# A transformer block with experts on one core: the causal mask moved to GpSimd, second expert product turned, token step and first expert rearranged

## The reference, cut to what matters

```python
h = concatenate([tok(x), txt], axis=1)                 # (32, 165, 256)
n = layernorm(h)
q, k, v = heads(n @ Wq + bq), heads(n @ Wk + bk), heads(n @ Wv + bv)
att = einsum('bhtd,bhsd->bhts', q, k) / sqrt(16)
att = where(key <= row and key % 4 != 3, att, -inf)
h = h + merge(softmax(att) @ v) @ Wp + bp
xn = rmsnorm(layernorm(h)) * norm_weight               # (5280, 256)
probs = softmax(xn @ router_w.T + router_b)
gates, idx = top_k(probs.T, 660)                       # per expert
hmid = gelu(xn[idx] @ fc1_w.T + fc1_b)                 # (8, 660, 1024)
ye = hmid @ fc2_w.T + fc2_b                            # (8, 660, 256)
out = scatter_add(ye * gates) / sum of a token's gates
h = h + out
```

## Time and profile before

| | us |
|---|---|
| median of 3 runs | 911.26 (909.67 to 915.45) |
| the profiled execution | 917.64 |
| its span | 915.8 |
| PE busy | 781.5 (85%) |
| DVE busy | 626.4 (68%) |
| ACT busy | 336.8 (37%) |
| POOL busy | 290.2 (32%) |

### The profile page before, as it was taken

One profiled execution on the slowest core, in us unless ns is written; L12 is line 12 of the kernel. 1 busy time (PEld: TensorE's weight loads), 2 busy tenths in 40 slices (PEclk: granted clock), 3 DMA queues, 4 the chain that ended last, 5 costly groups with the idle time before them and its releaser, 6 DMA issues. The chain is left out here.

```text
span 915.8 us, 19773 instructions
## 1 busy us (share of the span) xinstructions
PE 781.5 (85%) x7384; PEld 712.9 (78%) x7384; DVE 626.4 (68%) x1487; ACT 336.8 (37%) x729; POOL 290.2 (32%) x312
## 2 busy tenths in 40 slices
PE   4789999999999999989998621259999999999997
PEld 2668888888888888878887421259989998999997
DVE  1326768777677686776866567767877877878662
ACT  0203433343343333333332136116346264472560
POOL 3011122121221212222111120431653835637434
PEclk8879999999999999999999855559999999999999
DMA  9954574654765546644464170210442633415122
GB/s 296 260 80 62 65 114 89 94 77 83 114 99 87 83 84 103 108 78 80 84 98 72 45 242 0 92 31 13 95 127 26 147 96 60 131 23 101 31 30 31
DMA packets 81645, 83.22 MB, mean 91 GB/s; under 512 B 36249, under 2 KB 75911, under 8 KB 81212
## 3 DMA queue, kind: packets, MB, share of 16 engines
q1 hardware_dynamic: 68948, 67.82, 37.5%
q0 software_dynamic: 11584, 10.96, 7.7%
q10 hardware_dynamic: 1032, 3.37, 1.1%
HBM read 35.56 MB, written 16.22 MB: 57 GB/s over the span
## 5 line engine op out<-in xcount | busy, mean ns | idle before, releaser
L622 ACT ACTIVATE r_arena<-ps_all 126x660 f32<-126x660 f32 x128 | 92.3, 721 | 109.3 <-PE ps_all L815 109.3
L1166 DVE TENSOR_REDUCE mx<-ps_all 128x4 f32<-128x504 f32 (+1 forms) x160 | 104.7, 667 | 23.2 <-PE ps_all L791 22.8
L1177 DVE RECIPROCAL r_arena<-ps_all 128x165 f32<-128x165 f32 x64 | 76.1, 1189 | 57.1 <-PE ps_all L830 57.0
L541 POOL DMA_INDIRECT xe<-xn_rows,r_arena x48 | 69.4, 1446 | 133.2 <-DVE r_arena L1452 105.9
L1058 PE MATMUL ps_all<-W_hi,hT_hi 128*110 128x256 f32 x384 | 108.9, 284 | 0.0
L1058 PE MATMUL ps_all<-W_hi,hT_lo 128*110 128x256 f32 x384 | 107.7, 280 | 0.0
L1058 PE MATMUL ps_all<-W_lo,hT_hi 128*110 128x256 f32 x384 | 107.6, 280 | 0.0
L815 PE MATMUL ps_all<-Qp,Kp 98*126 98x166 f32 x512 | 102.5, 315 | 0.0
L554 POOL DMA_INDIRECT out<-r_arena x48 | 88.6, 1846 | 38.2 <-issue 35.8
L791 PE MATMUL ps_all<-Kp,Qp 96*65 96x56 f32 (+1 forms) x512 | 92.2, 297 | 0.0
L1490 DVE TENSOR_TENSOR hT_lo<-r_arena,hT_hi 128x330 fp32r<-128x330 f32 x128 | 63.3, 502 | 41.0 <-ACT r_arena L699 40.8
(11 more groups left out here) (172 smaller groups left out, 1821.6 us busy)
## 6 DMA issues: line engine op xcount, KB each, us to landing
H<-w SPq DMA_DIRECT2D x16, 1024.0 KB, 6.5
Qp<-q_hi SPq DMA_DIRECT2D x64, 166.0 KB, 3.9
Kp<-k_hi SPq DMA_DIRECT2D x128, 63.0 KB, 4.1
Qp<-q_lo SPq DMA_DIRECT2D x32, 166.0 KB, 4.5
out<-H SPq DMA_DIRECT2D x16, 330.0 KB
xn_rows<-r_arena SPq DMA_DIRECT2D x16, 330.0 KB
Kp<-k_lo SPq DMA_DIRECT2D x64, 63.0 KB, 4.0
H<-h SPq DMA_DIRECT2D x1, 3360.0 KB, 25.5
```

Source lines behind the costliest of these rows:

```text
L541: pool.indirect_dma_start(xe[0:A, a, :], None, xn_rows, bass.IndirectOffsetOnAxis(tok[0:A, u, a:a + 1], 0), bounds_check=NTOK - 1).then_in ...
L622: act.activation(PT[0:S, g, :, :].rearrange("p (k h) t -> p k h t", k=2), pair[:, :, :, 0:T], ACT.Exp, scale=float(HD) ** -0.5).then_inc(e ...
L1166: dve.tensor_reduce(dst, src, AX.X, ALU.max).then_inc(max_ready, 1)
L1177: dve.reciprocal(rS[:, c, :], bank(2 + c)[:, T:2 * T]).then_inc(rs_sum, 1)
```

## The change

- Masks: `mask_keys` and its products are gone from `key_scores`. On GpSimd `zero_future(b, g)`, an `affine_select` over `PT`, zeroes the entries of future keys after the exponential; `mix_values` waits for it (`causal_done`) and no longer for the exponential itself.
- Second products turned: `fc2` holds 128x128 pieces of W2 and streams 330 columns of the hidden rows, four quarters of 24 products (half j, features c). ACT adds the bias while it copies a quarter to `yS` (`evacuate`), PE transposes back (`output_rows`, three tiles after the third quarter, three after the first two blocks of the next expert's fc1), and DVE only multiplies by the slot weight.
- Token numbers: `slot_values(e+1)` comes after two of 16 blocks and `tokens(e+1)` after two features (`SV_AT = 1`).
- First expert: high and low parts of its weights are made in search steps 3 to 8; `first_tokens` starts with each third of the one-hots; gathers signal in two halves (for every expert), and `fc1(0)` takes the first half of the rows for four features first (`hidden_order`).
- The biases `b2` come with `vecs`, the eight broadcast loads on SP are gone; `pack_max` stands ahead of `store_h` on SP; PE's and ACT's expert loops are written out.

```diff
-SV_AT, TOK_AT = 4, 6
+SV_AT, SV_AT_FIRST = 1, 4
+def hidden_order(e):
+    if e == 0:
+        return [(f, j) for j in range(2) for f in range(KFF // 2)] + \
+               [(f, j) for f in range(KFF // 2, KFF) for j in range(2)]
+    return [(f, j) for f in range(KFF) for j in range(2)]
...
+            def zero_future(b, g):
+                pool.wait_ge(exp_done, 4 * b + g + 1)
+                apart(pool)
+                pool.affine_select(PT[0:S, g, :, :], PT[0:S, g, :, :], [[0, 4], [STEP - 1, T]], ALU.is_ge, 0.0,
+                                   base=STEP - 2, channel_multiplier=-STEP).then_inc(causal_done, 1)
...
+                if 3 <= step < 3 + KD:
+                    k = step - 3
+                    act.wait_ge(w1_in[0], 16)
+                    act.activation(W1_hi[:, k, :], W1[:, 0, k, :], ACT.Copy).then_inc(w1_hi_ready, 1)
+                if 3 + KD <= step < 3 + KD + KFF // 2:
...
             def mix_values(b, c):
-                pe.wait_ge(exp_done, 4 * b + 2 * c + 2)
+                pe.wait_ge(causal_done, 4 * b + 2 * c + 2)
...
+            def fc2(e, quarters):
+                for q in quarters:
+                    j, c = q // 2, q % 2
...
+                    for i, (w, h, f) in enumerate(terms):
...
+                        mm = pe.matmul(bank(4 + c)[:, 0:HALF], w[:, f, c * 128:(c + 1) * 128], h[:, f, cols],
                                        start=(i == 0), stop=(i == len(terms) - 1))
...
+            for e in range(NE):
+                split = 2 * (SV_AT if e else SV_AT_FIRST)
+                fc1(e, range(0, 2))
+                if e >= 1:
+                    output_rows(e - 1, range(3, NA))
+                fc1(e, range(2, split))
+                if e + 1 < NE:
+                    slot_values(e + 1, True)
+                fc1(e, range(split, 2 * KFF))
+                fc2(e, range(0, 2))
+                if e + 1 < NE:
+                    expert_transposes(e + 1, range(0, 2))
+                fc2(e, range(2, 3))
+                output_rows(e, range(0, 3))
+                if e + 1 < NE:
+                    expert_transposes(e + 1, range(2, 4))
+                fc2(e, range(3, 4))
+            output_rows(NE - 1, range(3, NA))
...
-                    hidden(e, u, seen, range(0, TOK_AT))
+                    hidden(e, u, seen, range(0, 1))
+                    weigh(e - 1, v, range(3, NA), e > 1)
+                    hidden(e, u, seen, range(1, SV_AT + 1))
                     tokens(e + 1, v, again)
-                    hidden(e, u, seen, range(TOK_AT, KFF))
+                    hidden(e, u, seen, range(SV_AT + 1, KFF))
```

More of the change, by code:

```diff
@@ L499, in _ @@
                 n, u = divmod(b, 2)
+                has_s = 0 <= b < B
                 if u == 0:
@@ L718, in _ @@
-            act.wait_ge(h_ready, 16 * (NE - 1))
-            gelus(NE - 1)
+                for n, (f, j) in enumerate(hidden_order(e)):
+                    act.wait_ge(fc1_done, 16 * e + n + 1)
+                    apart(act)
+                    if 16 * e + n >= 4:
+                        act.wait_ge(h_ready, 16 * e + n - 3)
+                        apart(act)
+                    act.activation(hT_hi[:, f, j * HALF:(j + 1) * HALF], bank(n % 4)[:, 0:HALF], ACT.Gelu,
+                                   bias=b1_s[:, e, f:f + 1]).then_inc(gelu_done, 1)
+                    act.activation(h_raw[:, n % 4, :], bank(n % 4)[:, 0:HALF], ACT.Gelu,
+                                   bias=b1_s[:, e, f:f + 1]).then_inc(gelu_done, 1)
@@ new lines, in evacuate @@
+            def evacuate(e, quarters):
+                for q in quarters:
+                    j, c = q // 2, q % 2
+                    act.wait_ge(fc2_done, 4 * e + q + 1)
+                    if e >= 1 and c == 0:
+                        act.wait_ge(yt_done, NA * (e - 1) + 3 * j + 3)
+                    act.activation(yS[:, c, j * HALF:(j + 1) * HALF], bank(4 + c)[:, 0:HALF], ACT.Identity,
+                                   bias=b2_s[:, e, c:c + 1]).then_inc(y_evac, 1)
+            act.activation(warm[:, :], kf("row"), ACT.Gelu)
@@ L1031, in fc1 @@
                 if 0 in parts:
[L1032 removed]
+                    pe.wait_ge(xeT_ready, 4 * e + 2)
                     pe.wait_ge(w1_split, KD * e + KD)
[L1034 to L1045 removed]
@@ L1062, in _, with output_rows @@
+            def output_rows(e, tiles):
+                for a in tiles:
+                    at_bank, at_col = y_place[a]
+                    if a % 3 == 0:
+                        pe.wait_ge(y_evac, 4 * e + 2 * (a // 3) + 2)
+                    for c in range(KD):
+                        mm = pe.transpose(bank(at_bank)[0:A, at_col + c * 128:at_col + (c + 1) * 128],
+                                          yS[:, c, a * A:(a + 1) * A], ident)
+                    mm.then_inc(yt_done, 1)
             first_tokens()
```

258 lines of the change are left out of this document (122 added, 136 removed).

## The result

The changed kernel takes 917.91 us (median of 20 runs, 914.74 to 921.89); the kernel before, 913.51 in 20 runs beside it (909.67 to 919.82). The ratio is 1.0049, with a 95% interval of 1.0030 to 1.0068: half a per cent slower, inside the 1% that the prediction takes for no change. The forecast was 897, 14 us faster. The profiled execution took 917.84 us, its span is 916.1.

What follows compares the result with a forecast made beforehand. PE was taken to bound attention's even rounds and the experts, DVE the odd rounds. -12.8 +1.0 +1.2 -7.2 +0.5 +3.5 = -13.8 us took 917.64 to 904, and the median 911.26 to 897; range 868 to 930.

Steps and rivals of the forecast that it cites:

- Masks and the end of attention: Attention: mask products replaced by GpSimd selects, -12.8 us over 16 pairs of rounds; last round's norm-weight products behind selects, +1.0.
- The 0.3 us by which selects hold DVE: Odd attention rounds: GpSimd selects block DVE's two-port ops, adding 0.3 us to the DVE chain.
- the 0.35 us of the odd round: Odd attention rounds: PE waits 0.35 us for the last select before the second half of the mixing products.
- Search: Threshold search: GpSimd's low parts of the first expert's weights hold DVE there, net +1.2 us, bounds 0 to +6.
- the token products: First expert: 16 of 48 token products start behind each third of the one-hots, 32 beside DVE: -3.1 us.
- The rest of the first expert: First expert: fc1 on half the rows -1.3 us, slot values and early gather -0.3, fc2 by quarters -2.5.
- fc1 starts on half the rows: First expert: fc1 starts on half the rows, without the second half's low parts: -1.3 us.
- Experiments 1 to 6: No such term in the prediction.
- PE waits 3.3 us. Everything won is gone: Experts 1 to 6: the token step waits for an earlier scatter; PE's 3.3 us wait leaves +0.1 an expert.
- The last expert and the end: PE ends 1.1 us earlier, but six late scatters queue on GpSimd and lengthen the end by 4.7: +3.5 us.
- the missing token wait: Rival, experts 1 to 6: no wait for the scatter, six experts each 3.3 us shorter, 877 us; chance 0.20.
- The slow select: Rival, attention: selects of 1.4 us become the bound, attention +29 us, 939 us; chance 0.25.

Runs made afterwards that it cites:

- experiment 8: The changed kernel with three buffers of token numbers, but masks as before (a mask product on PE per bank, no select on GpSimd): 895.07 us.
- late conversions: Three-buffer kernels with the high parts of the first expert's weights made after the search, as in the kernel before; without further change 876.87 and 880.85 us.
- experiment 10: Three-buffer kernel with the first expert's hidden products in the other experts' order, each block for both halves of its rows: 881.50 us.
- experiment 11: The changed kernel with three buffers of token numbers, run again beside the one with the first expert's high parts after the search: 879.17 us.
- three buffers: The changed kernel with three instead of two buffers of token numbers and slot weights in turn: 881.43 us, ratio 0.965 to the kernel before.
- experiment 5: The changed kernel with PE repeating one hidden product four more times before its wait in experts 1 to 6: 904.93 us, ratio 0.990.
- Experiments 7: Three-buffer kernel in which the last expert turns output tiles 0 to 2 before its third quarter of second products: 881.00 us.
- experiment 9: Three-buffer kernel, first expert's high parts after the search, last expert's second products in column parts of 330, 220 and 110: 876.97 us.
- experiment 4: The kernel before with only the masks changed: no mask products, selects on GpSimd, the queue's new order: 898.91 us, ratio 0.983.
- experiment 2: The changed kernel, two buffers, with SV_AT = 3, so slot values and token step come later in an expert: 892.82 us, ratio 0.977.

## Why the prediction was wrong

The forecast was -13.8 us; the spans differ by +0.3 and the medians by +4.4. Step by step, with the forecast's terms first:

- *Masks and the end of attention*, -12.8 +1.0 = -11.8: measured -14, the right size, in part by luck. The view of the pair of rounds, with DVE as the limit, was right, and a pair went from 28.22 to 27.22 us where -0.8 was forecast. Its parts were not: the reciprocals show -0.2 us in an odd round and -0.8 in an even one, not +0.3 and -1.1. The mask products filled 0.86 us of a round and not 1.3. The select was 0.77 us, not 1.0, between my two figures from the copies (0.67 and 0.97). The 0.3 us by which selects hold DVE is not there (21.03 us of DVE in a pair, with and without them). PE waited for a select twice, 1.0 us in all, and its weight loads 5.3 us in all, as they had for the exponentials before (5.2), so the 0.35 us of the odd round is not a new wait either.
- *The baseline.* I took the profiled execution, 6.4 us above the median, and carried the difference on. That surplus did not carry: the changed kernel's profiled run (917.84) stands at its median. The trace of before had lost 7.1 us ahead of its first full round, by a late arrival of packed keys and the lowered clock behind it (experiment 8). So of the 21.4 us by which attention looks shorter, 14.3 are the change. Five other traces, with and without the broadcast loads of b2, start late in the same way, so the late start is not the b2 loads alone; whether they make it more frequent was not tried.
- *Search*, +1.2, and the token products, -3.1: together -1.2 (70.65 to 69.50 us from the search to the transposes). The token products gave 3.0 (1.67 for 4.65), as worked out, so the search cost 1.8, and the traces with late conversions give 1.9. The forecast's 1.2 was the right size.
- *The rest of the first expert*, -4.1: measured -2.7 (43.72 to 41.07). The step that failed is "fc1 starts on half the rows: -1.3"; experiment 10 shows 0. By the clock in fc1 this stretch varies: it is 41.07 us in the changed kernel and 42.6 in experiment 11.
- *Experts 1 to 6*, +0.5: measured +20.6. **This is where the prediction fell.** The arithmetic of the work was right: -3.2 an expert was forecast without the wait, and three buffers show 34.24 against 37.33, -3.1. The wait was found, with its place and its mechanism, and at 3.3 us it was 0.8 too small (4.1). What failed is the sentence "PE waits 3.3 us. Everything won is gone": it priced a stand at its own length. PE's stand also lowered its clock, and fc1 behind it took 9.90 us for 7.33; experiment 5 shows that this goes when PE keeps working: of the 2.4 us an expert and 14.6 in six, 1.2 in six are left. -3.1 +4.1 +2.4 = +3.4 an expert. I had read that PE waited 2.13 us for gathered rows while its products kept their 0.153 us, and did not ask what a longer stand would do, though the first expert's 0.29 us products showed the price.
- *The last expert and the end*, +3.5: measured +4.9. Of the sum the tail was too small: the span ends 12.5 us behind the last product (903.6 to 916.1), not 11.1, because the fourth scatter starts 2.44 us after its weighing (904.90 to 907.34), where the first starts after 1.53. Experiments 7 and 9 have the same 2.44 with GpSimd idle for 4 us. Why stays open.

Against the medians the parts, -14 -1.2 -2.7 +20.6 +4.9 = +7.6, are 3.2 us above the measured 4.4. Executions of one kernel vary by as much through the same clock effect: six experts of the old code by 4.4 us (experiment 4), the start of attention by 4 to 7. This is enough to hold the rest, but no run assigned it.

Of the rivals, the missing token wait is what three buffers built: its 877 us are the 879 to 881 measured there. The slow select was far off (0.77 against a deciding 1.2). The full masks could not have paid 42 us: the products filled 27.5.

## What to carry to other kernels

Price a new wait of PE in two parts, its length and what the products behind it cost at half clock: 4.1 us of waiting cost 6.5 here. When a step is moved ahead to hide one transfer, ask which buffer it writes and whose transfer still reads that buffer; a third small buffer (12 words a row here) was worth 37 us of 918. And take a sum's baseline from several executions: the one profiled run had lost 7 us at its start that others of the same attention code do not lose.

## What the runs showed of the hardware that I had not expected

- After a stand of 4 us the granted clock was at its lower level and stayed there some 5 us into the work; in the experts of before, with waits of at most 2.2 us, it had stayed at 1.00 (first row of the two stretches above); in experiment 4 it fell behind waits of 2.76 and 2.19 us, in experiment 2 it stayed behind 2.31. At the start of attention it fell behind 1.42 us in one trace and stayed at 1.00 behind 1.44 us in another. Useless work in place of the stand made the kernel 13 us faster (experiment 5).
- A select with one operand over 126x660 takes 0.77 us, less than at the copies' rate for its columns (0.97), and eight of them in a pair of rounds leave DVE's busy time at 21.03 us; a two-operand subtraction holds DVE's op on one column for 2.3 us.
- A product of 110 columns costs as much as one of 220, 0.110 us, against 0.153 for 330 (experiment 9). The Trainium skill, page "TensorE: Matmul & The Clock Gate", section "Back-to-back issue gap", says that the spacing is set by the weight load and the product together, so that narrow products gain less than their columns; the trace agrees (each of these loads 128x128 weights).
